# Values of a windowed attention by row tiles: 64 keys by 96 queries a product, four tiles side by side, in two parts

## The chip, the cores and the metric

The kernel runs on one core of a Trainium2 chip. The metric is the device time of one execution in microseconds; the median of three runs is compared. Five engines work side by side, each through its own instructions in order, and wait for each other by semaphores: PE (TensorE, matrix products, into the accumulator memory PSUM), ACT (ScalarE), DVE (VectorE), POOL (GpSimd) and SP (SyncE, which here only issues DMAs).

## What is computed

Four sequences of 512 tokens by 128 channels (x) pass a linear attention, a transformer block of six layers, a retention layer and the same transformer block again. Nearly all the time is in the two blocks of six layers. The part that matters, for one layer (the scales and the rotary tables left out):

```python
q, k, v = split(shift_tokens(x) @ Wqkv)      # 16 heads of 64
...
def local_attention(q, k, v):
    w = WINDOW                               # 32
    ...
    bk2, bv2 = (look(bk), look(bv))          # a window's keys: its own 32 and the 32 before
    sim = jnp.einsum('bhwie,bhwje->bhwij', bq, bk2) * QK_SCALE
    sim = jnp.where(mask, -jnp.finfo(sim.dtype).max, sim)
    attn = jax.nn.softmax(sim, -1)
    out = jnp.einsum('bhwij,bhwje->bhwie', attn, bv2)
...
for i in range(DEPTH):                       # 6
    x = attn_layer(shift_tokens(x), ...) + x
    x = ffn_layer(shift_tokens(x), ...) + x
```

The change is in the second einsum: the product of the softmax weights with the values.

## The kernel before

After the linear attention (some 235 us) the kernel goes through 49 steps. A step (`step(s, prev, cur)`, written once for each engine) handles one sequence in one layer, in two halves that overlap with the neighbours: the attention of the present sequence (`cur`), and the end of the attention, the output projection and the feed-forward part of the one before it (`prev`). The order of the work on every engine is written out by hand in `step`. 42 of the steps with both halves are plain; five in the middle (s = 22 to 26) also hold the retention layer and have an order of their own; the first step has no `prev`, the last no `cur`.

The 16 heads go in four quads g = 0 to 3 of four heads. In a step's text g is relative to the present sequence, so `values(-3)` is quad 1 of the sequence before, `values(-1)` its quad 3. For a quad:

- PE: `project(g, banks)` makes queries and keys, one PSUM bank each for four parts, three products a bank (L722 to L724); `project_v(i, tiles)` the values of two quads, a bank for each of four tiles of 128 tokens (L731 to L733). These banks rotate over three PSUM banks.
- ACT squares them (L1028) and scales them out of PSUM (L1029); POOL adds the squares (L1222); PE sums them (`norms`, L741, into the two banks `NO`); ACT takes logarithm and exponential in place (L1040, L1042); DVE makes the factors (L1287) and finishes the keys (L1291), POOL the queries (L1226, L1231), DVE having multiplied by the rotary table (L1277, L1282).
- PE: `mask_scores` and `scores` (L747, L752, then 64 small products, L762); DVE takes the maxima (L1297) and subtracts them (L1300), ACT exponentiates (L1046), DVE sums, inverts, scales (L1306 to L1312) and transposes in 32 by 32 blocks (L1315) into `pt`.
- SP: `weights(g)` copies `pt` to `tb` with eight DMAs (L587 to L592), so that the keys of a row tile of 128 stand on the 128 partitions and the query windows that look at them stand beside each other.
- PE: `values(g)` (L783), the work of the change; ACT (or DVE, L1338) copies the two `NO` banks to `ot` (`evacuate_out`, L1051). `norms` and `values` of all quads take turns in these two banks.
- PE: `project_out(g)` (L801) adds the quad's part of the output projection to bank 7. When quad 3 is in (`project_out(3)` in a plain step), DVE adds the residual (L1326), ACT shifts it (L1055, L1056), PE takes the mean (L807), and so on to the feed-forward products (L817, L824), which end the step.

A value product before has the 128 keys of a tile on the rows of PE's array, 64 columns for the 64 dimensions of a head, and 160 query columns (five windows; 128 for the last tile). Two heads stand side by side on the array's columns. All are f32, and the profile has two instructions for each f32 product: 16 products are `x32` there. A quad's products for its first two heads come first and end with `o_ready[0]`, then those of the other two with `o_ready[1]`.

Of the kernel before, what the change touches and what calls it, by code (L numbers as in the profile page):

```python
# [3 lines left out]
def build_hybrid(nc, x_in, tabs, wa, wb, wf, out):  # L4
# [13 lines left out]
    B, N = 4, 512  # L18
# [12 lines left out]
    with ctx:  # L31
# [352 lines left out]
        def order_of(ret1, ret2):  # L384

            if not ret1 and not ret2:
# [25 lines left out]
        o_read = [per_quad(f"o_read{i}", ahead=3) for i in range(2)]  # L412
        wo_ready, fs_done = Signal("wo_ready"), Signal("fs_done", 2)
# [17 lines left out]
                    *((8, c) for c in (-12, -8, -7, -6, -5, -4, -3, -2, -1, 0)), *((16, c) for c in range(-15, 1)),  # L431
# [7 lines left out]
        def stage_ffn():  # L439
            scope = ExitStack()  # L440
            with scope:
# [19 lines left out]
                tb = t("tb", [128, 5, 16, WIN])  # L461
# [59 lines left out]
                def _(sp):  # L521
# [33 lines left out]
                    def step(s, prev, cur, hidden_layer=None, next_layer=None, new_layer=None):  # L555
# [25 lines left out]
                        def weights(g):  # L581

                            sp.wait_ge(o_ready[1].sem, now.count(o_ready[1], g - 1))
                            sp.wait_ge(p_tr.sem, now.count(p_tr, g))
                            for r in range(4):
                                rows = slice(32 * r, 32 * r + 32)
                                sp.dma_start(tb[rows, r], ptb[rows, 1]).then_inc(t_dma.sem, 16)  # L587

                                if r:
                                    sp.dma_start(tb[32 * r - 32:32 * r, r], ptb[rows, 0]).then_inc(t_dma.sem, 16)  # L590
                                else:
                                    sp.dma_start(by_head(tb[96:128, 4])[:, :, 0:6], by_head(ptb[rows, 0])[:, :, 2:8]).then_inc(t_dma.sem, 16)  # L592
# [88 lines left out]
                def _(pe):  # L681
                    def step(s, prev, cur):
# [83 lines left out]
                        def values(g):  # L766

# [833 lines left out]
```

## Time and profile before

| | |
|---|---|
| median of three runs | 3267.26 us (3266.84 to 3269.28) |
| profiled execution | 3269.6 us, of which the span of its instructions 3267.8 us |
| granted TensorE clock, mean | 0.976 of full speed |
| busy, of the span | PE 3067.1 us (94%), DVE 2927.5 us (90%), ACT 2266.0 us (69%), POOL 1814.5 us (56%) |
| a plain step | some 61.3 us |

Busy time is the time in which an engine had an instruction under way. For PE it counts a product from its start to its modelled end, so products that follow each other overlap in it. The span begins with the first instruction of the profile and ends with the last; all times below are counted from its start.

### The profile page before, as it was taken

To read this page: it belongs to the slowest core of one execution; us is meant where nothing else is said; L and a number is where in the kernel's file an instruction comes from. 1 tells how busy PE (TensorE), PEld (TensorE's weight loads), DVE (VectorE), ACT (ScalarE), POOL (GpSimd) and SP (SyncE) were. 2 spreads that over 40 slices of the span, in tenths; PEclk is the share of its full clock that TensorE was granted. 3 is DMA by queue.
4 is the path that set the end of the run, shared out by engine and by line. 5 is a ranking of instruction groups with operands and counts; after the bars stand their busy time and mean duration, and the time that the engine had idled before them with its cause. 6 is when DMAs were issued, how large, how long until landed. Compare 5 with 4: busy or idle time off the path is not lost.

```text
span 3267.8 us, 93879 instructions
## 1 busy us (share of the span) xinstructions
PE 3067.1 (94%) x37848; PEld 1899.2 (58%) x37848; DVE 2927.5 (90%) x2712; ACT 2266.0 (69%) x3691; POOL 1814.5 (56%) x822
## 2 busy tenths in 40 slices
PE   5768999999999999999999999999999999999997
PEld 3535665565565565566566655665665655655663
DVE  4549999999999999999999999999999999999995
ACT  1136777777777777777666777777777777777774
POOL 5525555555555555555454555655655655656651
PEclk8778999999999999999999999999999999999998
DMA  5534454454454454455344445445445445445442
GB/s 174 185 99 113 105 147 118 105 147 118 104 146 119 104 145 121 103 144 141 87 120 107 104 105 145 121 103 145 120 103 146 119 105 146 117 106 146 115 117 57
DMA packets 254252, 398.01 MB, mean 122 GB/s; under 512 B 51132, under 2 KB 84984, under 8 KB 254136
## 3 DMA queue, kind: packets, MB, share of 16 engines
q1 hardware_dynamic: 254136, 396.48, 46.4%
q8 instruction: 71, 1.16, 0.2%
q14 instruction: 45, 0.37, 0.0%
HBM read 64.71 MB, written 19.92 MB: 26 GB/s over the span
## 4 chain that ended last, share of the span: by engine, by line
PE 39%; DVE 23%; ACT 19%; issue 9%; POOL 1%; SPq 1%; DMA 1%; DVEq 0%; ACTq 0%; POOLq 0%
PE ps L783 6%; PE ps L741 5%; PE ps L801 5%; PE ps L817 5%; PE ps L762 5%; PE ps L722 4%; DVE f_mx L1297 4%; ACT f_ab L1029 3%; DVE f_p L1300 3%; ACT f_u L1028 3%; DVE f_p L1312 3%; ACT ps L1040 3%; PE ps L724 3%; PE ps L723 3%; ACT f_p L1046 3%
## 5 line engine op out<-in xcount | busy, mean ns | idle before, releaser
L1226 POOL TENSOR_TENSOR f_w<-f_w,f_ab 128x1024 f32<-128x1024 f32 x192 | 549.0, 2859 | 527.3 <-DVE f_w L1277 527.3
L1231 POOL TENSOR_TENSOR f_ab<-f_w,f_rn 128x1024 f32<-128x1024 f32 x192 | 594.3, 3095 | 390.9 <-DVE f_rn L1287 374.1
L1222 POOL TENSOR_TENSOR f_u<-f_u 128x512 f32<-128x512 f32 x384 | 588.6, 1548 | 363.3 <-ACT f_u L1028 363.2
L1029 ACT ACTIVATE f_ab<-ps,f_pa 128x512 f32<-128x512 f32 x768 | 542.0, 706 | 1.2
L1028 ACT ACTIVATE f_u<-ps 128x512 f32<-128x512 f32 x768 | 467.0, 608 | 96.7 <-PE ps L724 91.5
L1277 DVE TENSOR_TENSOR f_w<-f_ab,f_tan 128x1024 f32<-128x1024 f32 x384 | 500.9, 1345 | 4.3 <-POOL f_ab L1231 2.3
L783 PEld LDWEIGHTS ps<-f_tb,f_v 128*64 128x64 f32 x6144 | 396.4, 138 | 102.7 <-issue 86.5
L783 PE MATMUL ps<-f_tb,f_v 128*64 128x160 f32 (+1 forms) x6144 | 442.7, 297 | 12.2 <-DMA f_tb<-f_pt 9.9
L1040 ACT ACTIVATE ps<-ps 128x512 f32<-128x512 f32 x384 | 204.7, 574 | 340.4 <-PE ps L741 340.1
L722 PE MATMUL ps<-f_xh,f_wh 128*128 128x512 f32 x768 | 380.7, 496 | 53.2 <-ACT f_ab L1029 43.7
L741 PE MATMUL ps<-f_u,f_ones 128*128 128x512 f32 x768 | 368.8, 601 | 6.1 <-POOL f_u L1222 5.1
L801 PE MATMUL ps<-f_ot,f_wout 128*128 128x512 f32 x768 | 366.4, 600 | 3.0 <-DVE zT L1346 2.9
L762 PEld LDWEIGHTS ps<-f_kb,f_qb 64*32 64x32 f32 x24576 | 269.1, 105 | 108.4 <-issue 105.5
L1306 DVE TENSOR_REDUCE f_rs<-f_p 128x16 f32<-128x1024 f32 x192 | 233.4, 1216 | 102.3 <-ACT f_p L1046 102.3
L1291 DVE TENSOR_TENSOR f_ab<-f_w,f_rn 128x1024 f32<-128x1024 f32 x192 | 316.0, 1646 | 6.6
L762 PE MATMUL ps<-f_kb,f_qb 64*32 64x64 f32 x24576 | 304.1, 226 | 3.5 <-issue 3.4
L1046 ACT ACTIVATE f_p<-f_p 128x1024 f32<-128x1024 f32 x192 | 202.6, 1055 | 148.9 <-DVE f_p L1300 148.5
L724 PE MATMUL ps<-f_xh,f_wl 128*128 128x512 f32 x768 | 304.5, 396 | 0.0
L723 PE MATMUL ps<-f_xl,f_wh 128*128 128x512 f32 x768 | 303.0, 395 | 0.0
L1312 DVE TENSOR_TENSOR f_p<-f_p,f_rs 128x1024 f32<-128x1024 f32 x192 | 290.2, 1511 | 1.9
L817 PE MATMUL ps<-f_fq,f_w 128*128 128x512 f32 (+1 forms) x576 | 274.3, 612 | 11.1 <-issue 3.6
L1315 DVE STREAM_TRANSPOSE f_pt<-f_p 128x1024 f32<-128x1024 f32 x192 | 239.1, 1245 | 20.9
(170 smaller groups left out, 4975.6 us busy)
## 6 DMA issues: line engine op xcount, KB each, us to landing
f_kb<-f_ab SPq DMA_DIRECT2D x384, 256.0 KB, 3.6
f_qb<-f_ab SPq DMA_DIRECT2D x384, 256.0 KB, 3.6
f_tb<-f_pt SPq DMA_DIRECT2D x1344, 64.0 KB
f_wh<-split_w SPq DMA_DIRECT2D x48, 384.0 KB, 4.4
f_wl<-split_w SPq DMA_DIRECT2D x48, 384.0 KB, 4.2
a_w_raw<-wqkv SPq DMA_DIRECT2D x24, 384.0 KB, 4.1
split_w<-a_w_hi SPq DMA_DIRECT2D x24, 384.0 KB, 2.3
split_w<-a_w_lo SPq DMA_DIRECT2D x24, 384.0 KB, 2.8
```

The source lines that it names most:

```text
L722: nc.tensor.matmul(bank("qk", g, i), wh[:, g, i, :], xh[:, :], start=True, stop=False)
L741: last = nc.tensor.matmul(ps[:, NO[i], :], ones[:, :], u[:, 2 * i + 1, :], start=True, stop=True)
L762: last = nc.tensor.matmul(ps[rows, SS[h], c0:c0 + 64], qb[dims, pair, w0:w0 + WIN], kb[dims, pair, w0:w0 + 2 * WIN], start=False, stop=Tru ...
L783: last = nc.tensor.matmul(ps[rows, NO[pair], 128 * tile:128 * tile + WIN * windows], v[:, tile, d0:d0 + 64], tb[:, 0:windows, 8 * (h % 2) ...
L801: last = nc.tensor.matmul(f, wout[:, 2 * g + i, :], ot[:, 2 * g + i, :], start=g + i == 0, stop=g + i == QUADS)
L817: nc.tensor.matmul(bank(kind, -1, j)[0:m], w1[:, first + 128 * j:first + 128 * j + m], fq[:, :], start=True, stop=True).then_inc(ready.sem, 1)
L1028: nc.scalar.activation(u[:, i, :], bank("qk", g, i), ACT.Square).then_inc(sq_done.sem, 1)
L1029: nc.scalar.activation(ab[:, g % 2, i, :], bank("qk", g, i), ACT.Identity, scale=pa[:, g, i:i + 1]).then_inc(qk_read.sem, 1)
L1222: nc.gpsimd.tensor_tensor(u[:, 2 * i + 1, :], u[:, 2 * i, :], u[:, 2 * i + 1, :], ALU.add).then_inc(sq_sum[i].sem, 1)
L1226: nc.gpsimd.tensor_tensor(w[:, 0:2, :], w[:, 0:2, :], ab[:, k % 2, 0:2, :], ALU.add).then_inc(q_sum.sem, 1)
L1231: nc.gpsimd.tensor_tensor(ab[:, k % 2, 0:2, :], w[:, 0:2, :], rn[:, 0:1, :].broadcast_to([128, 2, N]), ALU.mult).then_inc(rope_q.sem, 1)
L1277: nc.vector.tensor_tensor(w[:, a:4:2, :], ab[:, k % 2, 1 - a:4:2, :], tan2[:, a:a + 1, :].broadcast_to([128, 2, N]), ALU.mult).then_inc(tu ...
```

## The change

Each value product is cut into pieces of 64 keys (half the array's rows) by 64 dimensions by 96 query columns (three windows; two at the sequence's end). Four pieces stand side by side in the array: two halves of the keys by two heads. The two row halves of one moment write to different banks: a quad is done in two parts, and in part 0 the upper half of the keys of heads 0 and 1 goes to bank `NO[0]` while the lower half of heads 2 and 3 goes to `NO[1]`; in part 1 it is the other way round. Between the parts PE waits on a new semaphore, `o_part`, and at the head of each part a product of zeros of 8 columns over the whole array is new (`nothing`). `tb` shrinks from five to three windows a tile, with the same eight DMAs; SP now waits for both `o_ready`. In each step one other piece of PE's work is put between the two parts of a quad. Its core (the uses of a counter table and the retention steps' order left out):

```diff
+        o_part = per_quad("o_part", 2)
...
-                tb = t("tb", [128, 5, 16, WIN])
+                tb = t("tb", [128, 3, 16, WIN])
...
                         def weights(g):
-                            sp.wait_ge(o_ready[1].sem, now.count(o_ready[1], g - 1))
+                            for i in range(2):
+                                sp.wait_ge(o_ready[i].sem, now.count(o_ready[i], g - 1))
...
-                                sp.dma_start(tb[rows, r], ptb[rows, 1]).then_inc(t_dma.sem, 16)
+                                sp.dma_start(tb[rows, r % 2], ptb[rows, 1]).then_inc(t_dma.sem, 16)
...
-                        def values(g):
+                        def values(g, part):
+                            if part == 1:
+                                pe.wait_ge(o_part.sem, now.count(o_part, g))
+                                value_products(g, part)
+                                return
...
                             pe.wait_ge(t_dma.sem, now.count(t_dma, g))
                             pe.wait_ge(gain.sem, now.count(gain, at))
-                            for pair in range(2):
-                                for tile in range(TILES):
-                                    windows = 5 if tile < TILES - 1 else 4
-                                    for h in (2 * pair, 2 * pair + 1):
-                                        rows = slice(64 * (h % 2), 64 * (h % 2) + 64)
-                                        d0 = 256 * (g % QUADS) + 64 * h
-                                        last = nc.tensor.matmul(ps[rows, NO[pair], 128 * tile:128 * tile + WIN * windows],
-                                                                v[:, tile, d0:d0 + 64], tb[:, 0:windows, 8 * (h % 2) + 2 * tile + h // 2, :],
-                                                                start=tile == 0, stop=tile == TILES - 1, skip_group_check=True,
-                                                                tile_position=(0, 64 * (h % 2)))
-                                last.then_inc(o_ready[pair].sem, 1)
+                            value_products(g, part)
+
+                        def value_products(g, part):
+                            nothing = mask[:, 288:768:64]
+                            nc.tensor.matmul(ps[:, NO[0], 0:8], identb[:, :], nothing, start=part == 0, stop=part == 1, skip_group_check=True)
+                            for tile in range(TILES):
+                                for h in range(2):
+                                    for pair in range(2):
+                                        half = pair ^ part
+                                        at = 128 * tile + 64 * half
+                                        windows = 3 if at < N - 64 else 2
+                                        rows, d0 = slice(64 * half, 64 * half + 64), 256 * (g % QUADS) + 128 * pair + 64 * h
+                                        last = nc.tensor.matmul(ps[64 * h:64 * h + 64, NO[pair], at:at + WIN * windows],
+                                                                v[rows, tile, d0:d0 + 64], tb[rows, 0:windows, 8 * h + 2 * tile + pair, :],
...
+                                                                tile_position=(64 * half, 64 * h))
+                                        if part == 1 and tile == TILES - 1 and h == 1:
+                                            last.then_inc(o_ready[pair].sem, 1)
+                                        if part == 0 and tile == TILES - 1 and h == 1:
+                                            last.then_inc(o_part.sem, 1)
...
-                            values(-2)
-                        if cur:
-                            project_v(0, range(2, TILES))
+                            values(-2, 0)
+                        if cur:
+                            project_v(0, (2,))
+                        if prev:
+                            values(-2, 1)
+                        if cur:
+                            project_v(0, (3,))
...
                         if prev:
+                            values(-1, 0)
                             project_out(2)
-                            values(-1)
+                            values(-1, 1)
                         if cur:
                             mask_scores(1)
                         if prev:
                             project_out(3)
```

PE's order in a plain step, at quad 3 of the sequence before, first as it was: after the last product of `project_v` (L733) come `project_out(2)` (L801), `values(-1)` (L783), the mask (L747), `project_out(3)` (L801) and `norms(2)` (L741).

```order
L733 MATMUL ps<-f_wh,f_xl 128x512
L801 MATMUL ps<-f_ot,f_wout 128x512 x2
L774 REGISTER_ALU
L783 MATMUL ps<-f_tb,f_v 64x160 x6
L783 MATMUL ps<-f_tb,f_v 64x128 x2
L783 MATMUL ps<-f_tb,f_v 64x160 x6
L783 MATMUL ps<-f_tb,f_v 64x128 x2
L747 MATMUL ps<-f_mask,f_identb 128x512
L800 REGISTER_ALU
L801 MATMUL ps<-f_ot,f_wout 128x512 x2
L741 MATMUL ps<-f_u,f_ones 128x512 x2
```

The same place of the changed kernel, whose line numbers are its own (L736 for L733, L789 the product of zeros, L799 the value products, L820 for L801, L750 for L747, L744 for L741):

```order
L736 MATMUL ps<-f_wh,f_xl 128x512
L781 REGISTER_ALU
L789 MATMUL ps<-f_mask,f_identb 128x8
L799 MATMUL ps<-f_tb,f_v 64x96 x13
L799 MATMUL ps<-f_tb,f_v 64x64
L799 MATMUL ps<-f_tb,f_v 64x96
L799 MATMUL ps<-f_tb,f_v 64x64
L820 MATMUL ps<-f_ot,f_wout 128x512 x2
L789 MATMUL ps<-f_mask,f_identb 128x8
L799 MATMUL ps<-f_tb,f_v 64x96 x12
L750 MATMUL ps<-f_mask,f_identb 128x512
```

The first half of the value products now stands ahead of `project_out(2)`, and with it the wait for the DMAs that fill `tb`; before, the wait stood behind it.

At quad 2 of the sequence before, PE's order is now, from the last product of `project_v(0, range(2))` to `norms(1)` (L744):

```order
L736 MATMUL ps<-f_wh,f_xl 128x512
L780 REGISTER_ALU
L781 REGISTER_ALU
L789 MATMUL ps<-f_mask,f_identb 128x8
L799 MATMUL ps<-f_tb,f_v 64x96 x13
L799 MATMUL ps<-f_tb,f_v 64x64
L799 MATMUL ps<-f_tb,f_v 64x96
L799 MATMUL ps<-f_tb,f_v 64x64
L705 REGISTER_ALU
L734 MATMUL ps<-f_wh,f_xh 128x512
L735 MATMUL ps<-f_wl,f_xh 128x512
L736 MATMUL ps<-f_wh,f_xl 128x512
```

There the first part stands where the whole quad stood, and one tile of `project_v` (L734 to L736) follows before the second part; before, both tiles followed the whole.

## Rows read from the trace of the kernel before

**Rows 1.** Windows, one step: length; busy PE, loads, DVE, ACT, POOL (count); clock, DMA.

```profile
1008.60:1069.90 61.30, 59.55 (x774) 36.97 (x774) 57.67 (x54) 46.16 (x75) 35.83 (x16) 1.00 0.45 115
```

**Rows 2.** Timeline, DVE, that step: start, duration, engine and operation, count.

```profile
1031.99 1.25 DVE L1315 STREAM_TRANSPOSE f_pt<-f_p 128x1024 f32<-128x1024 f32 x1
...
1035.52 1.99 DVE L1291 TENSOR_TENSOR f_ab<-f_w,f_rn 128x1024 f32<-128x1024 f32 x1
1037.59 1.22 DVE L1297 TENSOR_REDUCE f_mx<-ps 128x16 f32<-128x1024 f32 x1
...
1045.80 0.65 DVE L1326 TENSOR_TENSOR f_x<-zT,ps 128x512 f32<-128x512 f32 x1
```

**Rows 3.** Timeline, POOL and ACT, that step; in brackets idle time and releaser.

```profile
1035.14 1.28 POOL L1222 TENSOR_TENSOR f_u<-f_u 128x512 f32<-128x512 f32 x1 [6.98 <-ACT f_u L1028]
...
1031.38 1.07 ACT L1040 ACTIVATE ps<-ps 128x512 f32<-128x512 f32 x2 [1.12 <-PE ps L741]
```

**Rows 4.** Timeline, PE, that step, up to the next step's mask.

```profile
1008.60 0.39 PE L747 MATMUL ps<-f_mask,f_identb 128*128 128x512 bf16 x1 [0.24 <-DVE f_p L1300]
...
1021.21 1.48 PE L762 MATMUL ps<-f_kb,f_qb 64*32 64x64 f32 x128
...
1025.43 0.39 PE L733 MATMUL ps<-f_wh,f_xl 128*128 128x512 f32 x1
1025.75 2.29 PE L783 MATMUL ps<-f_tb,f_v 128*64 128x160 f32 x32
1027.96 0.50 PE L731 MATMUL ps<-f_wh,f_xh 128*128 128x512 f32 x1
1028.30 0.40 PE L732 MATMUL ps<-f_wl,f_xh 128*128 128x512 f32 x1
1028.53 0.39 PE L733 MATMUL ps<-f_wh,f_xl 128*128 128x512 f32 x1
...
1029.47 1.88 PE L741 MATMUL ps<-f_u,f_ones 128*128 128x512 f32 x4
...
1038.79 1.88 PE L801 MATMUL ps<-f_ot,f_wout 128*128 128x512 f32 x4
1040.59 2.29 PE L783 MATMUL ps<-f_tb,f_v 128*64 128x160 f32 x32
1042.81 0.39 PE L747 MATMUL ps<-f_mask,f_identb 128*128 128x512 bf16 x1
1043.04 1.88 PE L801 MATMUL ps<-f_ot,f_wout 128*128 128x512 f32 x4
1044.76 1.88 PE L741 MATMUL ps<-f_u,f_ones 128*128 128x512 f32 x4
...
1069.93 0.39 PE L747 MATMUL ps<-f_mask,f_identb 128*128 128x512 bf16 x1 [0.24 <-DVE f_p L1300]
```

**Rows 5.** Groups, value products, whole span: busy, mean ns, idle before.

```profile
L783 PE MATMUL ps<-f_tb,f_v 128*64 128x160 f32 x4608 | 391.1, 305 | 12.2 <-DMA f_tb<-f_pt 9.9 <-DVE f_rn L1287 1.7 <-issue 0.4
```

**Rows 6.** Timeline, PE's weight loads (PEld): quads 2 and 3 of that step.

```profile
1025.75 2.05 PEld L783 LDWEIGHTS ps<-f_tb,f_v 128*64 128x64 f32 x32 [0.36 <-issue]
...
1040.59 2.05 PEld L783 LDWEIGHTS ps<-f_tb,f_v 128*64 128x64 f32 x32 [0.76 <-DMA f_tb<-f_pt]
```

**Rows 7.** Timeline, a step whose `tb` DMAs were issued late: mask to mask.

```profile
1192.59 0.39 PE L747 MATMUL ps<-f_mask,f_identb 128*128 128x512 bf16 x1 [0.23 <-DVE f_p L1300]
...
1210.03 2.05 PEld L783 LDWEIGHTS ps<-f_tb,f_v 128*64 128x64 f32 x32 [0.36 <-DMA f_tb<-f_pt]
...
1213.75 1.88 PE L741 MATMUL ps<-f_u,f_ones 128*128 128x512 f32 x4
...
1219.69 2.09 DVE L1291 TENSOR_TENSOR f_ab<-f_w,f_rn 128x1024 f32<-128x1024 f32 x1
...
1230.06 0.65 DVE L1326 TENSOR_TENSOR f_x<-zT,ps 128x512 f32<-128x512 f32 x1
...
1254.20 0.39 PE L747 MATMUL ps<-f_mask,f_identb 128*128 128x512 bf16 x1 [0.27 <-DVE f_p L1300]
```

More of the change, by code:

```diff
@@ L430, in build_hybrid @@
         PE_USES = [(1, -1), (1, 0), (1, 2), (2, -2), (3, -5), (3, -4), (3, -3), (3, 0), *((4, c) for c in range(-4, 1)),
-                    *((8, c) for c in (-12, -8, -7, -6, -5, -4, -3, -2, -1, 0)), *((16, c) for c in range(-15, 1)),
+                    *((8, c) for c in (-12, -10, -8, -7, -6, -5, -4, -3, -2, -1, 0)), *((16, c) for c in range(-15, 1)),
                     *((128, c) for c in range(-64, 33, 32)), *((512, c) for c in range(-640, -255, 128))]
@@ new lines, in value_products @@
+                        def value_products(g, part):
[10 more added lines that the diff above has]
+                                                                v[rows, tile, d0:d0 + 64], tb[rows, 0:windows, 8 * h + 2 * tile + pair, :],
+                                                                start=part == 0 and tile == 0, stop=part == 1 and tile == TILES - 1, skip_group_check=True,
+                                                                tile_position=(64 * half, 64 * h))
[3 more added lines that the diff above has]
+                                            last.then_inc(o_part.sem, 1)
@@ L890, in step @@
                             mask_scores(-1)
-                            project(0, (2, 3))
-                            values(-3)
+                            project(0, (2,))
+                            values(-3, 0)
+                            project(0, (3,))
+                            values(-3, 1)
                             ret_keys_by_queries()
@@ L926, in step @@
                             variance()
-                            project_v(1, range(2, TILES))
-                            values(0)
+                            project_v(1, (2,))
+                            values(0, 0)
+                            project_v(1, (3,))
+                            values(0, 1)
                             ret_values()
@@ L945, in step @@
                                 pe.wait_ge(split_first, 2)
-                            project(0, range(4))
+                            project(0, range(3))
+                        if prev:
+                            values(-3, 0)
+                        if cur:
+                            project(0, (3,))
                             if not prev:
@@ L950, in step @@
                         if prev:
-                            values(-3)
+                            values(-3, 1)
                             project_out(0)
@@ L971, in step @@
                         if prev:
+                            values(-1, 0)
                             project_out(2)
-                            values(-1)
+                            values(-1, 1)
                         if cur:
@@ L988, in step @@
                         if cur:
-                            project_v(1, range(2, TILES))
-                            values(0)
+                            project_v(1, (2,))
+                            values(0, 0)
+                            project_v(1, (3,))
+                            values(0, 1)
                             mask_scores(2)
```

11 lines of the change are left out of this document (7 added, 4 removed).

## The prediction

> **What bounds the kernel now.** I read the windows view of one step first. In 61.30 us PE is busy 59.55 and DVE 57.67 [rows 1]: two engines near full, so a saving on one is worth only what the other lets through. 42 of the 49 steps are of this plain kind, so a tenth of a microsecond in each is 4.2 us.
>
> The timelines say who waits for whom. At the head of the step PE's mask waits for DVE (idle 0.24 us, released by L1300), and again 61.33 us later [rows 4]: each step is tied to DVE's end of the one before. DVE's rows carry no idle time in brackets at L1291, L1297 or L1326 [rows 2]: DVE goes from one instruction to the next. Yet a late PE does lengthen the step, through POOL. L1291 at 1035.52 takes 1.99 us, and POOL's L1222, which started at 1035.14 with 1.28 us to run, ends at 1036.42: for 0.90 of the 1.99 us POOL's add is under way, and 1.09 us follow it. That add waited for ACT, and ACT's L1040 waited 1.12 us for PE's `norms(1)` [rows 3].
>
> The kernel contains the test of this. In one step of four the `tb` DMAs come late, and PE's `values(-2)` starts 17.44 us after the mask (1210.03 less 1192.59) in place of 17.15; `norms(1)` follows at 21.16 against 20.87, L1326 at 37.47 against 37.20, and the next mask at 61.61 against 61.33 [rows 2, 4, 7]. 0.29 us late on PE before `norms(1)` makes a step 0.28 us longer. I read it the other way too: earlier there, and the step is shorter, until something else comes last.
>
> **What the change saves on PE.** A quad's 32 instructions run two abreast: 16 rounds, 12 of 160 columns and 4 of 128, 2432 columns in all. An f32 instruction of 512 columns takes 0.43 us (four from 1043.04 to 1044.76 [rows 4]), 0.84 ns a column, so the stream is 2.04 us. The block takes 2.22 us from its start to the next product's (1025.75 to 1027.96, 1040.59 to 1042.81): 0.18 more. Around it are 0.32 us from L733 to the block where L732 to L733 is 0.23 (0.09 more), and 0.34 from L731 to L732 (0.11 more) [rows 4]. Edges: 0.38 us a visit, a quad 2.42 us.
>
> After the change a part has 32 instructions, four abreast: 8 rounds of 96 columns, 0.65 us. Each part is a visit of its own with 0.38 us of edges, and has the product of zeros. No row shows such a product. Above, it costs what the bf16 mask of 512 columns does, 0.23 us (1042.81 to 1043.04); below, about the spacing of the small products of L762, 1.48 us over 128, 0.01 us [rows 4]. With 8 columns it is nearest to the lower row: 0.02. A part is 1.05 us, a quad 2.10, and PE saves 0.32 us a quad, 1.3 us a step.
>
> That four tiles run abreast is not shown for this shape. L762, in tiles of 64 by 32, puts 128 instructions of 64 columns through in 1.48 us, where one at a time would take 128 times 0.054, 6.9 us [rows 4]: more than four abreast, row halves included.
>
> **Where it arrives: the first half of the step.** `values(-3)` and `values(-2)` both stand ahead of `norms(1)`: up to 0.64 us earlier. ACT can now empty both banks only when part 1 is done, which costs a little of it, and `norms(0)` may have to wait for POOL; I take 0.45 (bounds 0.3 and 0.64). By the 1:1 of rows 7 DVE then reaches L1326 at 1045.35 in place of 1045.80.
>
> **Where it is lost: the move past `project_out(2)`.** At quad 3 part 0 now stands ahead of `project_out(2)`, with its wait for `tb`. The loader idled 0.76 us before 1040.59, put down to the DMA, where the load at 1025.75 is put down to issue [rows 6]: `tb` landed between 1039.83 and 1040.59, while PE was in `project_out(2)` and lost nothing (9.9 us in the whole span went to this wait [rows 5]). Now PE is ready for part 0 at about 1038.79 less 0.45, 1038.3, and stands still until the landing. DVE's transposition L1315 at 1031.99, from which the DMAs start, lies before anything that became earlier, so the landing stays. PE idles 1.5 us a step here, more than the whole saving of the step.
>
> From the landing, its early end, the last wait of the residual is worked out: 1039.83; 0.15 for the release and the load of the zero product's weights; part 0, 1.05; `project_out(2)`, 1.72; part 1, 0.94 (the mask behind it has no 0.11); mask 0.23; `project_out(3)`, 1.72: 1045.64, where `norms(2)` starts. Before it was 1044.76 [rows 4]. So everything on PE from here is 0.88 us later. The last L801 ended at 1044.92 (1043.04 and 1.88) and L1326 started at 1045.80 [rows 2, 4]: its slack was 0.88 us. All of it is used up: L1326 starts at 1045.8 again, now released by PE, while DVE idles 0.45 us before it. Ends: with the zero product at 0.01 and nothing for the release, 1045.6, 0.2 us less a step; with the late end of the landing 0.76 more; with the zero product at 0.23, twice 0.21 more.
>
> The rest of the step follows L1326 as before. PE has two quads' parts less in it, but its mask waits for DVE.
>
> **Sum.** Plain steps: 0.05 us longer each (the middle of the sum and the leftover slack, slightly on the late side since most bounds lie there), 42 times: +2. In the last step `project_out(2)` moves behind the wait for `tb` with nothing else to do: 1.72 less 0.32, +1.4. The five retention steps have other work at this place, and DVE is as full: 0. Together +3.5 on the profiled execution's 3269.6 us; the median of the runs is 2.3 lower, 3267.3, so 3271 us. What a measurement tells from no change here is about 0.2%, 6.5 us.
>
> **Two rules of the Trainium skill.** The row is first: in `values` before, 32 loads take 2.05 us beside 32 products in 2.29 [rows 4, 6], so the load of one column tile runs beside the product of the other, in the same rows. "TensorE: Matmul & The Clock Gate" (Part 3, The mechanism) says that a load overlaps products under way only when its row group differs. By it, four tiles in two row groups would wait at each load; with the page's 64/1.2 = 53 ns for one, a round would be 0.134 us in place of 0.081, a part 0.42 longer, and the estimate 42 times 0.84, 35 us, above mine. The trace disagrees with it, so I hold it at 0.03.
>
> **Rivals.**
> - *The saving arrives* (0.21). The landing isn't last, or the residual's slack is larger than I read. For it: rows 7, with 1:1. Against it: 1.05, 1.72, 0.94 and 1.95 us of PE's work stand in a row behind a DMA that lands after 1039.83. 42 times 0.45 less, with the +1.4: 3250 us.
> - *Rows share a loading path* (0.10; slower). The weights of the upper and lower half are loaded one after the other. L762 doesn't exclude it: eight tiles in 16 rounds make 0.093 us a round, so a load of 32 columns has up to 0.046 if two follow each other, one of 64 up to 0.093, and a round up to 0.19. At the 0.135 of a round before (2.22 over 16, less edges), a part is 0.43 us longer, and with two parts behind the landing a step 0.9: 3309 us. It decides from 0.081 us a round on.
> - *Two abreast only* (0.04). Rounds double: a part 1.70 us, the step 1.3 longer: 3326 us. L762 speaks against it.
> - *A dearer visit or a later landing* (0.20; slower). 0.2 to 0.7 us more a step, from the bounds above, or DVE meets POOL once more in a step (0.9 us at L1291 is the price of such a meeting): +8 to +29, about 3285 us.
> - *No change* is the rest, 0.42: 3261 to 3274 us.
>
> **Chances and range.** Below 3261: the first rival, 0.21. Within: 0.42. Above: the other three, 0.34, and the rule's case, 0.03. The range takes in the first rival at its foot and the dearer visit at its top, and leaves out most of what lies beyond: 3248 to 3298 us.
>
> **What would show it.** PE idle before L789 or L799 at quad 3, released by the DMA of `tb`, about 1.5 us a step and 50 to 60 in all, against 9.9. A part at 1.05 us from start to next start with its product of zeros, with a round every 0.08 us. L1040 after `norms(1)` 0.45 us earlier from the mask, L1291 shorter by about as much. DVE idle before L1326 0.3 to 0.5 us, released by PE, in the plain steps. PE busy time less by some 60 us. Wrong is the prediction if DVE has no idle time before L1326 and the step is shorter (the first rival), or if a part takes 1.4 us or more (the second and third).

## The result, and the profile after

The changed kernel takes 3377.16 us (median of 4 runs, 3368.64 to 3384.50), the kernel before 3267.05 us beside it: ratio 1.0336, 95% interval 1.0303 to 1.0368. It is slower by 110 us. The prediction, 3271 us with a range of 3248 to 3298, was wrong.

The diff adds lines, so L722 to L807 of before stand at L725 to L826, DVE's and ACT's lines 37 further down (L1291 is L1328, L1326 is L1363, L1051 is L1088). `values` is L799 now, its product of zeros L789, `project_out` L820. These are lines of the page of the changed kernel: busy times, the queue of instruction fetches (packets, MB, share), and the chain by engine.

```profile
PE 2993.3 (89%) x44136; PEld 1806.1 (54%) x44376; DVE 2907.1 (86%) x2712; ACT 2261.4 (67%) x3691; POOL 1813.8 (54%) x822
...
q8 instruction: 444, 7.27, 0.9%
...
PE 28%; DVE 26%; ACT 17%; issue 9%; SPq 9%; DMA 4%; POOL 1%; DVEq 0%; ACTq 0%; POOLq 0%
```

PE's busy share fell from 94% to 89%. How much less PE does can't be read from the 2993.3: this trace lacks the records of 240 mask products (44136 products beside 44376 weight loads). The trace of e2, the same instructions and the same loss, has them all and shows 3063.8 us, 3 less than before; what half clock costs is in that number too. The page of before has 71 packets of instructions, and 1% each for SPq and DMA in its chain. The groups of the changed kernel (busy, mean ns of one, then idle time before them and what ended it):

```profile
L820 PE MATMUL ps<-f_ot,f_wout 128*128 128x512 f32 x768 | 395.9, 640 | 34.3 <-ACT f_ot L1088 30.4 <-DVE zT L1383 3.6
L1328 DVE TENSOR_TENSOR f_ab<-f_w,f_rn 128x1024 f32<-128x1024 f32 x192 | 297.3, 1548 | 6.6
L789 PE MATMUL ps<-f_mask,f_identb 128*128 128x8 bf16 x384 | 70.1, 183 | 97.6 <-DMA f_tb<-f_pt 86.9 <-issue 8.4 <-DVE f_rn L1324 1.4
L1363 DVE TENSOR_TENSOR f_x<-zT,ps 128x512 f32<-128x512 f32 x48 | 32.9, 686 | 109.6 <-PE ps L820 109.6
```

The last line is the loss: DVE stands idle for 109.6 us in all before the residual, until `project_out(3)` releases it; in before it is 13.7 us. The two above it name two causes. `values` waits 86.9 us for `f_tb` (9.9 in before [rows 5]), and `project_out` waits 30.4 us for ACT's evacuation of the outputs (3.0 us of idle time in all, none of it by ACT, in before).

One step on PE, at quad 3, and the DVE instructions that go with it:

```profile
989.06 0.18 PE L789 MATMUL ps<-f_mask,f_identb 128*128 128x8 bf16 x1
989.17 0.88 PE L799 MATMUL ps<-f_tb,f_v 64*64 64x96 f32 x32
989.99 0.50 PE L734 MATMUL ps<-f_wh,f_xh 128*128 128x512 f32 x1
...
1003.95 0.18 PE L789 MATMUL ps<-f_mask,f_identb 128*128 128x8 bf16 x1 [1.77 <-DMA f_tb<-f_pt]
1004.07 0.89 PE L799 MATMUL ps<-f_tb,f_v 64*64 64x96 f32 x32
1004.88 3.68 PE L820 MATMUL ps<-f_ot,f_wout 128*128 128x512 f32 x4
1008.37 0.20 PE L789 MATMUL ps<-f_mask,f_identb 128*128 128x8 bf16 x1
1008.50 0.89 PE L799 MATMUL ps<-f_tb,f_v 64*64 64x96 f32 x32
1010.08 1.98 PE L820 MATMUL ps<-f_ot,f_wout 128*128 128x512 f32 x4 [0.69 <-ACT f_ot L1088]
1011.90 1.88 PE L744 MATMUL ps<-f_u,f_ones 128*128 128x512 f32 x4
```

```profile
995.29 1.25 DVE L1352 STREAM_TRANSPOSE f_pt<-f_p 128x1024 f32<-128x1024 f32 x1
...
1012.37 0.69 DVE L1363 TENSOR_TENSOR f_x<-zT,ps 128x512 f32<-128x512 f32 x1 [3.40 <-PE ps L820]
```

The first three rows time a part: 0.93 us from its start to the next product (989.06 to 989.99), the product of zeros 0.11 of it. The rows behind the dots are those of quad 3, and three things stand out in them. Part 0 waits 1.77 us for `f_tb`. `project_out(3)` waits 0.69 us for ACT. And `project_out(2)` takes 3.49 us from its start to the next product, where it took 1.80 before (1038.79 to 1040.59 [rows 4]). The windows view of these stretches says why (length, PE busy, then granted clock, DMA share and GB/s):

```profile
1003.95:1004.88 0.93, 0.93 (x34) 1.00 0.99 192
1004.88:1008.37 3.49, 3.49 (x8) 0.52 0.53 136
1008.37:1009.20 0.83, 0.83 (x34) 0.98 0.95 200
1010.08:1011.90 1.82, 1.82 (x4) 1.00 0.38 83
```

The granted clock is 0.52 in `project_out(2)`: 1.2 GHz in place of 2.4. The trace's clock record has 19 stretches at half clock after the first 400 us in the changed kernel, 4 in before. Of the 19, 3 stand at the kernel's end; the other 16 stand at this place, 15 of them in the 42 plain steps. The other plain steps pass it at full clock, though PE waits there too (1.63 us on average, against 1.92 in the steps with half clock).

And SP's queue has rows such as these (start, duration of the issue of one transfer):

```profile
1285.31 0.59 SPq L590 DMA_DIRECT2D f_tb<-f_pt  x1
1285.94 2.74 SPq L593 DMA_DIRECT2D f_tb<-f_pt  x1
1288.72 0.59 SPq L590 DMA_DIRECT2D f_tb<-f_pt  x1
```

One issue took 2.74 us among issues of 0.59. Two fetches of 16 KB of code had started just before it, at 1285.74 and 1285.86, and took 1.03 and 2.45 us, so they ran beside it. Between 300 and 3100 us the changed kernel has 43 issues for `f_tb` of over 1.5 us, before has 5. In the window 1000 to 1400 us, plain steps alone, before has no packet of instructions, the changed kernel 61 (packets, MB, share):

```profile
q1 hardware_dynamic: 31085, 46.04, 45.8%
q8 instruction: 61, 1.00, 1.1%
```

### The profile page after: what moved, and what is told of

It is laid out like the page before. It is cut to its first block, busy times and chain, and to the rows that moved or that the text cites. A ratio compares the mean times of both kernels' runs of the same rounds, so it can differ in the third digit from the quotient of the medians.

```text
span 3366.9 us, 106809 instructions
## 1 busy us (share of the span) xinstructions
PE 2993.3 (89%) x44136; PEld 1806.1 (54%) x44376; DVE 2907.1 (86%) x2712; ACT 2261.4 (67%) x3691; POOL 1813.8 (54%) x822
## 4 chain that ended last, share of the span: by engine, by line
PE 28%; DVE 26%; ACT 17%; issue 9%; SPq 9%; DMA 4%; POOL 1%; DVEq 0%; ACTq 0%; POOLq 0%
PE ps L820 9%; DVE f_w L1314 6%; SPq L590 5%; DMA f_tb<-f_pt 4%; PE ps L799 4%; ACT f_ab L1066 3%; ACT f_u L1065 3%; PE ps L836 3%; DVE f_p L1349 3%; DVE f_rs L1343 3%; PE ps L744 3%; SPq L593 2%; DVE f_pt L1352 2%; PE ps L765 2%; ACT f_p L1083 2%
## 5 line engine op out<-in xcount | busy, mean ns | idle before, releaser
L725 PE MATMUL ps<-f_xh,f_wh 128*128 128x512 f32 x768 | 381.9, 497 | 97.0 <-ACT f_ab L1066 44.2
L820 PE MATMUL ps<-f_ot,f_wout 128*128 128x512 f32 x768 | 395.9, 640 | 34.3 <-ACT f_ot L1088 30.4
L744 PE MATMUL ps<-f_u,f_ones 128*128 128x512 f32 x768 | 373.8, 607 | 9.9 <-POOL f_u L1259 6.8
L799 PE MATMUL ps<-f_tb,f_v 64*64 64x96 f32 (+1 forms) x12288 | 347.8, 249 | 0.1
L1088 ACT ACTIVATE f_ot<-ps 128x512 f32<-128x512 f32 x336 | 185.6, 600 | 215.4 <-PE ps L799 215.3
L1328 DVE TENSOR_TENSOR f_ab<-f_w,f_rn 128x1024 f32<-128x1024 f32 x192 | 297.3, 1548 | 6.6
L799 PEld LDWEIGHTS ps<-f_tb,f_v 64*64 64x64 f32 x12288 | 275.4, 134 | 34.0 <-issue 27.2
```

The source lines that it names most:

```text
L725: nc.tensor.matmul(bank("qk", g, i), wh[:, g, i, :], xh[:, :], start=True, stop=False)
L744: last = nc.tensor.matmul(ps[:, NO[i], :], ones[:, :], u[:, 2 * i + 1, :], start=True, stop=True)
L799: last = nc.tensor.matmul(ps[64 * h:64 * h + 64, NO[pair], at:at + WIN * windows], v[rows, tile, d0:d0 + 64], tb[rows, 0:windows, 8 * h + ...
L820: last = nc.tensor.matmul(f, wout[:, 2 * g + i, :], ot[:, 2 * g + i, :], start=g + i == 0, stop=g + i == QUADS)
```

## Experiments

Three times are followed in each, all counted from the start of DVE's transposition of quad 3 (L1315, L1352) and averaged over 38 plain steps of the run's trace. "Landing" is the arrival of the last of the eight `f_tb` transfers: 7.85 us in before, 8.63 in the changed kernel. "PE's end" is the end of the last product of `project_out(3)`: 13.01 and 15.70 us. "The residual" is its start on DVE (L1326, L1363): 13.86 and 15.99 us. The plain step goes with the residual: 61.42 and 63.96 us.

Wherever DVE waited for PE, the residual started 0.29 to 0.30 us after PE's end (e6, e9, the changed kernel). In before it starts 0.85 us after it, straight behind DVE's own work. So PE's end has 0.55 us of slack there: the residual moves only once PE's end lies beyond about 13.56 us.

**e1: longer code.** A filler ahead of every group of projections in the loops:
```
+ def filler():
+     if not isinstance(s, int):
+         for _ in range(24): pe.wait_ge(masked, N_MASKED)
```

 Theory order (the changed kernel's loss is all in its waits: both banks ready together, values ahead of the output product): no more packets than before, and 3267-3285, the waits' own dispatch. If there are packets and yet under 3285, fetching is harmless and order keeps the whole loss.

Measured: 3698.21 us, ratio 1.1315 (1.1288 to 1.1342), 407 packets. The packets came as expected, but the time is far over both expectations, because the waits stood on PE's own path: PE has 66% of the chain, issue 12%. The time says nothing of fetching. It gives a by-product: 288 more instructions in each of the 39 looped steps cost 430 us, fetching included, about 0.04 us for each instruction.

**e2: loop heads aligned.** Padding ahead of PE's two loops puts their first instruction at the start of a block of code; the body stays the same.
```
+ if eng.engine == mybir.EngineType.PE:
+     eng.addr_align(256, offset=0, max_nops=0)
  with eng.Fori(1, RET1) as s:
```

> The changed kernel, with the heads of TensorE's two loops placed at the start of a 16 KB block of code (padding that is branched over; no instruction of the body changes): its body of about 1886 instructions of 64 bytes then lies in 8 blocks and not in 8 or 9. Theory code with room for 8 blocks: packets of the instruction queue fall from 444 to under 120, and the time falls by 50 to 110 us, to 3270-3325, what is left being the order's. Theory code with room for fewer than 8 usable blocks: packets stay at 400 or more and the time within 0.3% of 3377. Theory order: packets may fall, the time stays at 3365-3380.

Measured: 3375.18 us, ratio to before 1.0324 (1.0306 to 1.0341), 416 packets. A body of 1886 instructions in 8 blocks doesn't stay either, so this settles nothing on what fetching costs.

**e3: both banks late.** The first bank's signal moves behind the last product of the quad:
```
- last.then_inc(o_ready[pair].sem, 1)
+ if pair == 1 and tile == TILES - 1:
+     last.then_inc(o_ready[h - 2].sem, 1)
```

> The kernel before, but the first bank of a quad's values is given to ScalarE only with the second, when the quad is done (about 1.2 us later than now), as the changed kernel must. Theory order, first term (the output product of the last quad waits for the evacuation of both banks: 30.4 us at its line in the changed kernel, 3.0 before): 20 to 30 us more, 3287-3297, with 25 us or more of idle time at project_out on ACT's evacuation and VectorE's f_x update waiting for it. Theory code, or the rival that the product has slack: within 8 us of 3267. No more instruction packets than 71 in either.

Measured: 3273.68 us, ratio 1.0013 (1.0003 to 1.0022). PE does wait for ACT (16.3 us at `project_out`), and PE's end comes at 13.60 us, 0.59 later; but that costs 5 us, not 20 to 30. The slack of 0.55 us takes nearly all of it: the residual comes at 13.89. Alone this term is small.

**e4: values first.** `values(-1)` ahead of `project_out(2)`.

> The kernel before, with values(-1) ahead of project_out(2) in the plain steps, where the changed kernel has its first part. Theory order, second term (TensorE then waits for the landing of f_tb with nothing to do, 1.5 us a step as I forecast, of which the chain to VectorE's f_x update takes 0 to 0.9 us): 0 to 40 us more, likeliest +10. If the landing is hidden: within 5 us of 3267 and the idle time at values <-DMA f_tb no larger than before (12.2 us). No more instruction packets than 71.

Measured: 3294.84 us, ratio 1.0082 (1.0065 to 1.0099). `values` waits 45.7 us for `f_tb`. PE's end comes at 14.06 us and the residual at 14.36; DVE waits 33.9 us before it.

**e5 and e6: short code in both kernels.** The scores are computed by half as many products, e5 in the kernel before and e6 in the changed one, so that both bodies stay on the engine. The scores are other numbers then, and the output is wrong; e14 and e15 build on e6 and share this.
```
- ps[rows, SS[h], c0:c0 + 64],  kb[dims, pair, w0:w0 + 2 * WIN]
+ ps[rows, SS[h], c0:c0 + 128], kb[dims, pair, k0:k0 + 128]
```

> The kernel before, with the scores as half as many products of 128 key columns instead of 64 (what two products of a window computed is replaced by one of the same number of columns, so the scores are other numbers): TensorE's loop body falls from 1612 to some 1100 instructions. It is the arm to compare e6 with. All theories: 71 packets or fewer, 3150 to 3267.

> The changed kernel with the same shortening of the scores as e5 (again other numbers): its body falls from 1886 to some 1374 instructions, less than that of the kernel before, and nothing of the order is touched. Theory code: packets in the loops are gone (under 110 in all), and its distance to e5 is what e3 and e4 together give, +15 to +45 us, instead of the change's +110. Theory order: packets gone as well, but the distance to e5 stays at 90 to 120 us.

Measured: 3248.01 us (ratio to before 0.9943) and 3330.31 us (1.0193, 1.0178 to 1.0208); 49 and 61 packets. With no fetching in the loops the change still costs 82 us. So the theory that code is most of the loss falls: it is left with the 28 us between 82 and 110. e6's group of the residual:

```profile
L1363 DVE TENSOR_TENSOR f_x<-zT,ps 128x512 f32<-128x512 f32 x48 | 32.9, 685 | 100.6 <-PE ps L820 100.5
```

Its landing is at 7.84 us, as in before, where the changed kernel's is at 8.63; and only one of e6's issues for `f_tb` takes over 1.5 us between 300 and 3100 us. So the late landings, at least, are the fetching's.

e6 also shows the chain of quad 3 with no other disturbance. These are its rows in a step at full clock, on PE and then DVE's residual:

```profile
1121.45 0.18 PE L789 MATMUL ps<-f_mask,f_identb 128*128 128x8 bf16 x1 [2.01 <-DMA f_tb<-f_pt]
1121.56 0.89 PE L799 MATMUL ps<-f_tb,f_v 64*64 64x96 f32 x32
1122.38 1.98 PE L820 MATMUL ps<-f_ot,f_wout 128*128 128x512 f32 x4
1124.20 0.18 PE L789 MATMUL ps<-f_mask,f_identb 128*128 128x8 bf16 x1
1124.30 0.89 PE L799 MATMUL ps<-f_tb,f_v 64*64 64x96 f32 x32
1125.88 1.98 PE L820 MATMUL ps<-f_ot,f_wout 128*128 128x512 f32 x4 [0.69 <-ACT f_ot L1088]
```

```profile
1128.17 0.69 DVE L1363 TENSOR_TENSOR f_x<-zT,ps 128x512 f32<-128x512 f32 x1 [1.40 <-PE ps L820]
```

From the start of part 1 to `project_out(3)` it is 1.68 us (1124.20 to 1125.88). In 22 of the 38 steps PE runs at full clock here, and PE's end is at 14.28 us; in the other 16 a stretch at half clock falls on `project_out(2)`, and PE's end is at 15.97. The steps are then 62.2 and 63.8 us long: 16 steps by some 1.65 us are 26 us.

**e7: as many instructions by cutting products.**
```
+ for c in range(len(cuts) - 1):
+     cols = slice(cuts[c], cuts[c + 1])
      nc.tensor.matmul(bank("qk", g, i)[:, cols], w[:, g, i, :], x[:, cols], ...)
```

> The kernel before with the projections cut into pieces of columns (in the loops: queries and keys 3 pieces, values 2, the sums of squares 2), the same columns and the same order: the body grows from 1612 to about 1884 instructions, as many as the changed kernel has. Theory code: 350 to 450 packets, idle time before the projections and before the output product that ended in nothing but issue, later landings of f_tb, and 40 to 100 us more. Theory order: packets, but 3267 to 3290 (only what 136 more pieces cost TensorE, 0.02 us or less each of dispatch, some of it beside its waits).

Measured: 3382.74 us, ratio 1.0354, 407 packets. PE's busy time rose to 3176.5 us and it has 64% of the chain: the cut products cost PE its own time, as the filler did. So it settles nothing on fetching.

**e8: row tiles in two quads.** `values(-3)` and `values(-2)` in parts, `values(-1)` and `values(0)` whole:
```
  project(0, range(3)); values(-3, 0); project(0, (3,)); values(-3, 1)
  ...
  values(-2, 0); project_v(0, (2,)); values(-2, 1); project_v(0, (3,))
  ...
  project_out(2); values(-1)
```

> Row tiles in two of the four quads alone: values(-3) and values(-2) in two parts at the changed kernel's places, values(-1) and values(0) whole and where before has them, f_tb laid out as before. Body about 1748 instructions. Theory code plus order: if 1748 stay on the engine (packets under 120), neither term of the loss is left, and the first half's gain that I forecast (0.32 us of TensorE a quad, 0.45 us a step by way of norms(1)) has to show: 3240 to 3266. If 1748 don't stay: 350 packets or more and 3300 or more. Rival (row tiles themselves cost, wherever they are): half of the change's 110 us, 3310 to 3330, without more packets.

Measured: 3279.22 us, ratio 1.0035 (1.0020 to 1.0050). There are 392 packets: 1748 instructions don't stay where they lie here. Yet the loss is 11 us, where I had written 3300 or more for that case. The runs spread more than others (3268 to 3290 over ten).

**e9: the order alone.** The products of before, in the changed kernel's order round quad 3, signals as in e3:
```
- project_out(2); values(-1)
+ values(-1, (0,)); project_out(2); values(-1, (1,))
```

> The kernel before, its products untouched (128 rows of keys, 160 query columns), but in the changed kernel's order round the last quad: first bank of values(-1), project_out(2), second bank, and both banks given to ScalarE at the quad's end. Theory order: e3 gave +5 and e4 +26 alone, but here nothing but mask_scores(1) stands between the last product and project_out(3), so TensorE waits for the evacuation of a bank behind a product that started late: 70 to 95 us more (3340 to 3363), project_out idle some 30 us on ACT f_ot, VectorE's f_x update idle 80 to 110 us behind it. Rival (the loss needs row tiles, by their zero products, their parts or their loads): the sum of e3 and e4 at most, 3285 to 3305.

Measured: 3329.84 us, ratio 1.0191 (1.0174 to 1.0208), a little under the expected range, well over the rival's. These are its rows on PE at quad 3, and DVE's residual:

```profile
994.06 1.25 PE L788 MATMUL ps<-f_tb,f_v 128*64 128x160 f32 x16 [0.82 <-DMA f_tb<-f_pt]
995.25 1.98 PE L807 MATMUL ps<-f_ot,f_wout 128*128 128x512 f32 x4
997.16 1.25 PE L788 MATMUL ps<-f_tb,f_v 128*64 128x160 f32 x16
...
999.10 1.98 PE L807 MATMUL ps<-f_ot,f_wout 128*128 128x512 f32 x4 [0.36 <-ACT f_ot L1058]
```

```profile
1001.38 0.69 DVE L1333 TENSOR_TENSOR f_x<-zT,ps 128x512 f32<-128x512 f32 x1 [1.21 <-PE ps L807]
```

So the order alone costs 62 us with no row tile in the kernel. The two terms cost 5 and 26 us alone and 62 together, because they share one slack: PE's end comes at 13.01, 13.60, 14.06 and 14.97 us in before, e3, e4 and e9, the residual at 13.86, 13.89, 14.36 and 15.26, and the time is up by 0, 5, 26 and 62 us. Up to about 13.5 us a later PE's end costs next to nothing; beyond, each 0.1 us costs 4 to 5 us, which is 0.1 us in each of the 42 plain steps.

**e10: `project_out(2)` back, the rest as changed.**
```
- values(-1, 0); project_out(2); values(-1, 1)
+ project_out(2); values(-1, 0); values(-1, 1)
```

> The changed kernel with project_out(2) ahead of both parts of values(-1) in the plain steps, as before has it; all else as changed. Theory order: the loss of this place goes, 3377 falls to 3280-3305 (what stays is e3's evacuation term and the fetching of code, if that costs anything), f_x's wait falls from 110 us to 15-30. Theory code, in its strong form (fetching delays TensorE and the landing of f_tb by 50 us or more): 3330 or more with 400 packets. Rival (parts abreast of nothing are dear): 3350 or more.

Measured: 3293.40 us, ratio 1.0081 (1.0064 to 1.0097), with 439 packets. One call moved takes off 84 us. It is 84 and not the 57 that lie between e9 and e3: the stretches at half clock are gone from the plain steps as well (5 in all after the first 400 us, where the changed kernel has 19).

**e11: e8 aligned.** The edit of e2 on e8.

> e8 (row tiles in two quads, body about 1748 instructions = 6.8 blocks of 256, 392 packets, 3279) with TensorE's two loop heads at the start of a block, so that the body touches 7 blocks and not 7 or 8. If 7 blocks stay on the engine and 8 don't (1612 instructions stayed, 1884 in 8 aligned blocks did not): packets under 120, and the time shows what fetching costs two kernels that are otherwise one: 0 to 15 us less than e8. If fewer than 7: 350 packets and e8's time.

Measured: 3252.11 us, ratio 0.9949 (0.9932 to 0.9965): faster than before. 78 packets, none in the window 1000 to 1400 us, where e8 has these:

```profile
q1 hardware_dynamic: 31033, 47.13, 46.7%
q8 instruction: 59, 0.97, 1.1%
```

The loops have the same instructions, now in 7 blocks and no more by their count, and take 27 us less (18 to 39 by the ends of the two intervals); I had expected 0 to 15. The landing is at 7.88 us against e8's 8.90 at quad 3, and at 7.88 against 10.29 at quad 1. Between 300 and 3100 us 3 issues for `f_tb` take over 1.5 us, where e8 has 63. So fetching costs 27 us here. That late `f_tb` is its way is what the trace suggests; no run delays the transfers alone.

**e12: row tiles in three quads.**
```
+ project_v(1, (2,)); values(0, 0); project_v(1, (3,)); values(0, 1)
```

> Row tiles in values(-3), values(-2) and values(0), in two parts as changed; values(-1) whole and where before has it. Body about 1816. Theory order (the loss is at values(-1) and project_out alone): within 8 us of e8's 3279, f_x's wait under 25 us. Rival (every quad by rows costs something, about a quarter of the 110 us): 3300 or more.

Measured: 3291.08 us, ratio 1.0085 (1.0066 to 1.0104), 413 packets. It is 12 us over e8 (16 by the ratios), between the two expectations. The trace puts it at quad 3 once more: `values(-1)` waits 26.5 us for `f_tb`, where e8's whole quads wait 8.4 in all, and DVE stands 25.7 us before the residual, where it stands 16.6 in e8. The landing is at 9.13 us against 8.90. Why it is later is not shown; e15 bears on it.

**e13: before aligned.** The edit of e2 on the kernel before.

> The kernel before with TensorE's two loop heads at the start of a block of code, as in e11. If e11's 14 us come from row tiles in two quads: within 0.2% of before, about 71 packets. If they come from the alignment: 3252 as e11.

Measured: 3266.36 us, ratio 0.9999 (0.9989 to 1.0008). So what e11 gains on before comes from the row tiles.

**e14: PE kept busy in the wait.** On e6, six products without use in `project_v(1)`, ahead of `values(-1, 0)`:
```
+ for _ in range(6):
+     nc.tensor.matmul(bank("v", i, tile), xh[:, cols], wh[:, pair, 4:6, :], start=True, stop=True)
```

> e6 (the changed kernel with short scores, 3330, 22 stretches at half clock after the first 400 us), with 6 more products of 512 columns (0.215 us each, into the bank of the value projection, which its own three products then overwrite) where TensorE waits 2.0 us for f_tb ahead of values(-1) in the plain steps. Theory clock (the idle time ahead of the first part is what lowers it): the stretches at half clock fall from 22 to about 5, as in e9, f_x's wait from 100 us to 65-75, and the time to 3298-3312, although the kernel does more. Rival (the clock falls by the row tiles' products themselves): stretches stay at 15 or more, 3325 or more.

Measured: 3303.44 us, ratio 1.0112 (1.0095 to 1.0129): 27 us less than e6 for more work, about the 26 that e6's own steps gave. PE's idle time ahead of part 0 falls from 1.94 to 0.60 us a step, the stretches at half clock from 22 to 7 (from 16 to 1 in the 38 plain steps), and DVE's wait from 100.6 to 76.1 us:

```profile
L1365 DVE TENSOR_TENSOR f_x<-zT,ps 128x512 f32<-128x512 f32 x48 | 32.9, 685 | 76.1 <-PE ps L822 76.1
```

**e15: e10 without fetching.**

> e6 with project_out(2) ahead of both parts of values(-1), as in e10: row tiles in all four quads, nothing fetched, half-clock stretches about 5. Theory sum (-14 of the first two quads, +12 of values(0), +5 of the late evacuation): 3245 to 3260, within 0.3% of e5's 3248, and the fetching of e10 (+27 against before) is then worth the difference, 20 to 30 us. Rival (row tiles in the last two quads are dear for themselves): 3275 or more.

Measured: 3238.01 us, ratio to before 0.9916 (0.9896 to 0.9935), 61 packets; e5, with the same scores, had 3248.01. It came out 7 us under my range. Row tiles in all four quads cost nothing where the order is before's and the code stays: they gain 10 us over e5. `project_out` waits 31.4 us for ACT here, more than the 30.4 of the changed kernel, and it costs nothing, since PE's end is at 12.75 us. With e10 it prices fetching again: e10 stands 27 us above before, e15 10 us below e5, 37 us between them. Of the three prices for fetching (27, 28 and 37 us) only e8 against e11 has the same instructions on both sides.

## Why the prediction was wrong, point by point

- **A part is 1.05 us, four tiles abreast: right, in mechanism and size.** From its start to the next product a part takes 0.93 us (989.06 to 989.99). With what it adds to its neighbours, 0.01 ahead of it and 0.10 behind (990.32 less 989.99 is 0.33, where 0.23 is usual), it is 1.04. (The prediction's last paragraph calls 1.05 the time "from start to next start"; by its own working 0.85 of it is that, with 0.09 ahead and 0.11 behind.) The rounds stand 0.08 us apart. PE's busy time is 65 us less in e15 than in e5, two traces that lack nearly as many mask records (240 and 238), for the 60 forecast. "Rows share a loading path" and "two abreast only" are out. So is the rule taken from the Trainium skill, "TensorE: Matmul & The Clock Gate", Part 3, that a load overlaps only where the row group differs: by it I had a part at 1.47 us. (The same section also lets a load go ahead into a background weight buffer; the prediction left that out.)
- **The first half gains 0.45 us a step: right in kind, 0.35 in size.** The L1291 that took 1.99 us [rows 2] takes 1.71 on average in e11 and 1.38 in e15 (1.72 in e5), and the step is shorter by 0.35 and 0.34 us (61.42 to 61.07, 61.11 to 60.77). In the changed kernel it takes 1.81, but there the residual waits for PE, and the gain is buried.
- **PE waits for `tb` at quad 3, 1.5 us a step: right.** It is 1.73 us in the plain steps, and 86.9 us in all in place of the 50 to 60 forecast; the landing itself came 0.8 us later than in before.
- **The chain from the landing to the residual: the step that failed.** I wrote part 1, mask, `project_out(3)` in a row, 1.17 us from part 1 to `project_out(3)`. The evacuation between them was left out: `project_out(3)` needs both banks of quad 3 in SBUF. In before half of that was done during the quad; now both banks are ready at its end, and only the mask stands between. The chain is 1.69 us in e6's steps at full clock, 0.52 more. And I let DVE start at the moment of PE's end, so I read the slack as 0.88 us; in the traces where DVE waits 0.30 us lie between them, so it was 0.55. These two terms, both put at nothing, are 0.8 us in each of the 42 plain steps. The smaller terms nearly cancel: `project_out(2)` takes 1.82 us, not 1.72 (rows 4 have 1.80 at this place), `project_out(3)` 0.10 more after its wait, and from the landing to `project_out(2)` it is 0.97, not 1.20. My sum put PE's end and the residual at 13.81 us; e6 has 14.28 and 14.58 at full clock. Nothing was left to take it in, so it was paid in every step: DVE idles 2.3 us before the residual on average (109.6 over 48), where I had 0.3 to 0.5. e9 shows it: +62 us for the order alone.
- **Not in the prediction: the clock.** In 15 of the 42 plain steps the granted clock is at half during `project_out(2)`, behind the wait for `f_tb` and part 0, and PE's end is 1.7 us later (e6). e14 filled most of the wait: 27 us. That it takes the idle time is shown. Whether it takes the row tiles too is not: e9, without them, has 4 such stretches, 3 of them at the kernel's end, but it also waits less (0.88 us a step on average, against 1.73). Why some steps have it and others, with the same rows ahead of it, do not is open.
- **Not in the prediction: the code.** By the trace's records PE's loop body grew from 1612 to 1886 instructions. I counted the instructions for PE's time and not for where they lie. 27 us (e8 against e11).
- **The other terms.** The retention steps were put at 0: from the last residual before them to the first behind them it is 419.0 us against 418.3, so that was right.

The sum against before is −14 (the gain, e11), +62 (order, e9), +27 (clock, e6 against e14) and +27 (code): 102 of the 110 us. A second sum stays nearer to this kernel: of the 82 us between e5 and e6 the clock has 27, which leaves 55 for the order with row tiles and their gain, and with the 27 of the code that is 109. The terms were each measured in another kernel, and they meet in one slack, so such sums are no closer than some 10 us. What stays open is e12's 12 us over e8. That the third quad costs them for itself is against e15; both fetch code, at other places of the step.

Of the rivals, "a dearer visit or a later landing" named the right place and part of the mechanism, with a price of 8 to 29 us against 110. Each of its items was bounded by a row of before. A wait that no row of before shows, because another order hid it, had no bound at all.

The best kernel found is e11: 3252.11 us, with row tiles in two quads and aligned loops, 0.5% faster than before.

## What to carry to other kernels

When a call moves in an engine's order, list what each later call waits for and ask what used to cover it: here the output product of quad 2, moved by one place, no longer covered the landing, and the evacuation lost its cover to the later signal. Work out the slack of the wait at the chain's end, from the releasing engine's end and with the time that a release takes; several small delays that each fit in it don't fit together. Compare busy times only between traces that have the same records. Before making a loop's body longer, look at the queue of instruction fetches in the loop: if it has no packets, the body stays on the engine, and that is worth keeping. Two alignment lines were worth 27 us, and the same two lines on a body that stayed anyway were worth nothing.

## What the runs showed of the hardware

- **Code that stays.** PE's loop bodies of 1612 instructions (before) and of 1748 with aligned loops (e11) brought no packets between 1000 and 1400 us; 1748 not aligned (e8) and 1886 aligned (e2) brought 59 and 56 packets of 16 KB, some 9 a step. The Trainium skill, "Runtime: NRT & Kernel Launch", section "Instruction fetch mechanics", gives PE 2048 instructions, filled in order in blocks of 16 KB or 256 instructions, says that a long kernel needn't fit, and that crossing a block is mostly hidden. Counted in such blocks, 7 aligned ones stayed here and 8 did not, fewer than the 2048. Nor was the refill hidden: it cost 27 us (e8 against e11), with one issue of SP at 2.74 us among others of 0.59 in the changed kernel, and the landings of `f_tb` 1.0 us later at quad 3 and 2.4 us at quad 1 (e8 against e11).
- **The clock.** The granted clock was 0.52 for 3.49 us after 1.77 us of idle time and one part by row tiles, at a place where the kernel before had PE in `project_out(2)` at full clock. There were 22 stretches at half clock with the idle time (e6), 7 with most of it filled (e14).
- **From PE to DVE.** The residual started 0.29 to 0.30 us after the end of PE's last product, wherever it waited for it (e6, e9, the changed kernel).
- **Row and column tiles together.** A part's 32 products of 64 rows, 64 columns of weights and 96 of data (some 64), f32, in four tiles: a round of four started every 0.08 us, and its loads ran beside the products (32 loads in 0.70 us, from 989.17 on, beside products in 0.88).
